# Eight key groups of the relu pass moved into the last head steps of the large pass

## What is computed

```python
x = x + xattn0(ln(x), ctx, Wq, Wkv, Wo, bo)       # 16 heads of 64 over 12544 context rows
x = x + band_attn(ln(x), ...)                     # self attention within a band
x = x + experts0(ln(x), ...)                      # 8 experts, the best 2
x = x + xattn1(ln(x), ctx, mask, W, b)            # below
x = x + scan(ln(x), ...)
x = x + experts1(ln(x), ...)                      # 32 experts and 2 shared ones

def xattn1(input, context, mask, W, b):           # the relu pass
    q = relu(input @ W.T + b)
    k = relu(context @ W.T + b)
    scores = where(mask, -inf, q @ k.T)
    return softmax(scores) @ k
```

## Time and profile before

| | us |
|---|---|
| median of 3 runs | 1534.51 |
| lowest and highest | 1531.64, 1535.97 |
| profiled execution | 1531.62 |
| its span, first to last instruction | 1529.9 |

### The profile page before, as it was taken

The page is one execution under the profiler, slowest core; times in us unless marked ns, Lnnn a source line. Parts: engine busy times, 40 slices in busy tenths (PEclk is TensorE's granted clock), DMA queues, the critical chain, the costliest instruction groups (busy, mean ns, idle before and its releaser), DMA issues. The chain is left out here.

```text
span 1529.9 us, 24927 instructions
## 1 busy us (share of the span) xinstructions
PE 1467.8 (96%) x9257; PEld 1272.2 (83%) x9257; DVE 1084.1 (71%) x2051; ACT 832.6 (54%) x1581; POOL 598.7 (39%) x517
## 2 busy tenths in 40 slices
PE   8999999999999999999999999999987979999769
PEld 6888888888888888888888888888875869999648
DVE  5777777777777777777777777777787337777784
ACT  4555566556555565556656566556652136666221
POOL 5243433434343434343434343343310245666240
PEclk9999999999999999999999999999999799999899
DMA  5000000000000000000000000000004221221720
GB/s 186 1 25 1 1 25 1 25 1 25 1 25 1 25 1 25 1 25 1 25 1 20 6 1 25 1 1 1 1 28 179 83 105 55 82 82 34 302 104 4
DMA packets 11099, 58.92 MB, mean 39 GB/s; under 512 B 2330, under 2 KB 4707, under 8 KB 9956
## 3 DMA queue, kind: packets, MB, share of 16 engines
q1 hardware_dynamic: 10980, 57.33, 10.0%
HBM read 57.19 MB, written 0.13 MB: 37 GB/s over the span
## 5 line engine op out<-in xcount | busy, mean ns | idle before, releaser
L487 DVE TENSOR_TENSOR pT<-ps,pT 128x896 fp32r<-128x896 f32 x224 | 244.5, 1091 | 203.8 <-ACT pT L396 203.8
L317 POOL CAST V<-Vraw 128x512 fp32r<-128x512 f32 x189 | 115.7, 612 | 651.1 <-ACT Vraw L402 550.5
L396 ACT ACTIVATE pT<-ps 128x896 fp32r<-128x896 f32 x224 | 205.9, 919 | 179.4 <-PE ps L562 178.6
L402 ACT COPY Vraw<-ps 128x512 f32<-128x512 f32 x189 | 110.9, 587 | 266.0 <-PE ps L544 266.0
L318 POOL TENSOR_TENSOR V<-Vraw,V 128x512 fp32r<-128x512 f32 x189 | 242.7, 1284 | 15.1
L433 DVE TENSOR_REDUCE nmx<-ps 128x1 f32<-128x896 f32 x224 | 242.0, 1080 | 0.0
L380 ACT ACTIVATE prob<-ps,nm 128x896 f32<-128x896 f32 x224 | 223.8, 999 | 0.0
L620 PE MATMUL ps<-ident,prob 128*128 128x128 f32 x1568 | 214.2, 277 | 8.7 <-ACT prob L380 4.5
L575 PEld LDWEIGHTS ps<-pT,V 128*128 128x128 f32 x1568 | 215.0, 188 | 8.1 <-issue 0.3
L575 PE MATMUL ps<-pT,V 128*128 128x256 f32 x1568 | 220.3, 280 | 0.0
L620 PEld LDWEIGHTS ps<-ident,prob 128*128 128x128 f32 x1568 | 167.5, 140 | 17.0 <-ACT prob L380 9.2
(11 more groups left out here) (312 smaller groups left out, 2426.7 us busy)
## 6 DMA issues: line engine op xcount, KB each, us to landing
raw<-in_ctxT SPq DMA_DIRECT2D x14, 896.0 KB, 4.4
d_raw<-in_ctxT SPq DMA_DIRECT2D x14, 896.0 KB, 4.6
w<-in_w SPq DMA_DIRECT2D x2, 4096.0 KB, 18.1
wg<-in_wg SPq DMA_DIRECT2D x1, 4352.0 KB, 17.8
wu<-in_wu SPq DMA_DIRECT2D x1, 4352.0 KB, 27.6
wd<-in_wd SPq DMA_DIRECT2D x1, 4352.0 KB, 36.3
e_ea<-in_alog SPq DMA_DIRECT2D x1, 2048.0 KB, 7.8
d_mrow<-in_mask SPq DMA_DIRECT2D x14, 112.0 KB, 4.5
```

Source lines behind the costliest of these rows:

```text
L317: link(pool, nc.gpsimd.tensor_copy(v_high(g, i), by_head(Vraw[:, j % 2, :])), "pool_chain")
L396: nc.scalar.activation(pT[u % 2][:, :, 0, :], pT_ps, ACT.Copy).then_inc(sem("pTh_ready"), 1)
L487: nc.vector.tensor_tensor(pT[u % 2][:, :, 1, :], pT_ps, pT[u % 2][:, :, 0, :].bitcast(F32), ALU.subtract).then_inc(sem("pTl_ready"), 1)
```

## The change

Eight of the 56 key groups of the relu pass (those of chunks 0 and 1) are made at the end of the large pass, with its own split chunks: chunks 0 and 1 are loaded and split once more as its chunks 14 and 15, the latter in quarters. Six groups go into bank 6 in steps 216 to 219, 222 and 223, the last two into banks 2 and 3 behind the projection and behind the last turned heads. For this the relu weights are loaded and split at the start of the kernel, with `Vraw` as the buffer, and `d_kT` becomes a ring of four. The relu pass starts with group 8 and has 13 groups before round 0, then three per round in rounds 0 to 8 and four in rounds 9 to 12. Chunks 2 and 3 are loaded in the band stage and split by GpSimd in the expert stage, where chunk 0 and the weights were; chunks 4 and 5 are loaded there. In the relu pass the first three turns of tiles come before groups 10 to 12, and VectorE's casts of the first keys before its other first work. Some constants are built later or in another place, `afc` is loaded in the band stage, and the numbers of spins change: 9 more in the band stage, 2 fewer in the first expert stage, 3 fewer in the last. The scan takes two buffers from `d_kT`.

```diff
@@ stage_context
+    LG = 2 * KT
+    later_at = [steps - 8, steps - 7, steps - 6, steps - 5, steps - 2, steps - 1]
+        wx_first = Vraw[:, 0, :].rearrange("p (k n) -> p k n", k=KT)
...
+                sp.dma_start(wx_first, t["wx"]).then_inc(sem("wx_early"), 16)
+                sp.dma_start(v["bx"][:, :], t["bx"]).then_inc(sem("wx_early"), 16)
...
-                for c in range(1, chunks):
+                for c in range(1, chunks + 2):
                     sp.wait_ge(sem("cT_split"), 2 * c)
-                    sp.dma_start(raw[:, :, :], t["ctxT"][c]).then_inc(sem("rawT_in"), 16)
+                    sp.dma_start(raw[:, :, :], t["ctxT"][c % chunks]).then_inc(sem("rawT_in"), 16)
...
+                pool.wait_ge(sem("wx_early"), 32)
+                link(pool, nc.gpsimd.tensor_copy(v["d_wxh"][:, :, :], wx_first), "pool_chain")
+                nc.gpsimd.tensor_tensor(v["d_wxl"][:, :, :], wx_first, v["d_wxh"][:, :, :].bitcast(F32),
+                                        ALU.subtract).then_inc(sem("wx_split"), 1)
                 split_context(1)
...
-                    elif u % H0 == H0 - 2 and u // H0 + 2 < chunks:
+                    elif u % H0 == H0 - 2:
                         split_context(u // H0 + 2)
+                split_quarters(chunks + 1)
@@ stage_context, ScalarE
+                def later_keys(G, bank):
+                    act.wait_ge(sem("dk_done"), G + 1)
+                    act.wait_ge(sem("wx_early"), 32)
+                    m, cols = (G % LG) // 2, slice((G % 2) * HK, (G % 2 + 1) * HK)
+                    nc.scalar.activation(v["d_kT"][G // LG][:, m, cols], ps[:, bank, 0:HK], ACT.Relu,
+                                         bias=v["bx"][:, m:m + 1], scale=1.0).then_inc(sem("dkT_ready"), 1)
...
+                    if u in later_at:
+                        later_keys(later_at.index(u), 6)
                     if u + 1 < steps:
                         exp_step(u + 1)
@@ stage_context, TensorE
+                    if u in later_at:
+                        pe.wait_ge(sem("o_added"), u - 1)
+                        pe.wait_ge(sem("vraw_ready"), len(v_steps))
+                        later_keys(later_at.index(u), 6)
                     p = u + AHEAD
...
+                        if u in later_at:
+                            pe.wait_ge(sem("dkT_ready"), later_at.index(u) + 1)
                         weighted_sum(u - 1)
...
                         project(range(0, 4))
+                        later_keys(6, 2)
...
                 weighted_sum(steps - 1)
                 turn_heads((4, 5, 6), 7)
+                later_keys(7, 3)
@@ stage_relu_context
-    done = [max(early, ahead)]
+    early, done = 8, [13]
+    SKIP = 2
     for c in range(chunks):
         left = chunks - 1 - c
-        share = -(-(groups - done[-1]) // left) if left > 0 else 0
+        share = (groups - done[-1]) // left if left > 0 else 0
...
+                for n in range(3):
+                    turn_keys(0, n)
                 for G in range(before, done[0]):
-                    relu_keys(nc, pe, sem, v, G, ps[:, G % 2, 0:HK])
-                for n in range(NG):
-                    if n == 3:
-                        pe.wait_ge(sem("dkNl_ready"), 1)
-                    turn_keys(0, n)
+                    keys(G)
                 pe.wait_ge(sem("dq_split"), 1)
                 scores(0)
+                pe.wait_ge(sem("dkNl_ready"), 1)
+                turn_keys(0, 3)
@@ stage_mix0, GpSimd
+                for i in range(2):
+                    pool.wait_ge(sem(f"dctx_in{i}"), 16)
+                    nc.gpsimd.tensor_copy(v["d_cTh"][i][:, :, :], v["d_raw"][i][:, :, :]).then_inc(sem("dcTh_ready"), 1)
+                    pool.wait_ge(sem("dcTh_ready"), i + 1)
+                    nc.gpsimd.tensor_tensor(v["d_cTl"][i][:, :, :], v["d_raw"][i][:, :, :],
+                                            v["d_cTh"][i][:, :, :].bitcast(F32), ALU.subtract).then_inc(sem("dcTl_ready"), 1)
-                v["spin"](8, 3)
+                v["spin"](6, 3)
@@ stage_band, TensorE (before the waits for o1, o1T and o2T)
+                v["spin"](3, 0)
+                v["spin"](3, 0)
+                v["spin"](3, 3)
@@ stage_mix1
-                v["spin"](8, 0)
+                v["spin"](5, 0)
```

More of the change, by code:

```diff
@@ L129, in build @@
         norms = (norm_vector, norm_pool, norm_tensor)
+        keep("bx", [P, KT])
+        keep("d_wxh", [P, KT, D], F32R)
+        keep("d_wxl", [P, KT, D], F32R)
+        v["d_kT"] = [sb(f"d_kT{i}", [P, KT, CK]) for i in range(2)]
         stage_context(nc, t, sb, sem, link, ps, norms, v)
+        keep("tri", [P, P])
+        keep("below", [P, E1, E1])
+        keep("afc", [P, KT, D])
+        keep("wx", [P, KT, D])
         keep("wg0", [P, KT, E0])
@@ L578, in weighted_sum, with later_keys @@
                     mm.then_inc(sem("pv_done"), 1)
+                def later_keys(G, bank):
+                    c = chunks + G // LG
+                    if G == 0:
+                        pe.wait_ge(sem("wx_split"), 1)
+                    if G % LG == 0:
+                        pe.wait_ge(sem("cT_split"), 2 * c + 2)
+                    if 0 < G < len(later_at):
+                        pe.wait_ge(sem("dkT_ready"), G)
+                    relu_keys(nc, v, G % LG, cTh[c % 2], cTl[c % 2], ps[:, bank, 0:HK]).then_inc(sem("dk_done"), 1)
                 def turn_heads(pairs, bank):
@@ L870, in stage_scan @@
         inv = [sb(f"e_inv{i}", [P, W], F32, own) for i in range(2)]
-        g = [sb(f"e_g{i}", [P, W], F32, own) for i in range(2)]
+        g = [x[:, :, :].rearrange("p k n -> p (k n)")[:, 0:W] for x in v["d_kT"][0:2]]
         def cn(x):
@@ L1084, in first_use @@
         return next((c for c in range(chunks) if done[c + 1] > KG * C), None)
-    to_split = {c: [C for C in range(chunks) if KG * C >= done[0] and max(first_use(C) - 1, 0) == c]
-                for c in range(chunks)}
+    to_split = {c: [C for C in range(2 + SKIP, chunks) if max(first_use(C) - 1, 0) == c] for c in range(chunks)}
     with ExitStack() as own:
@@ L1138, in load_mask @@
                         sem(f"dmask_in{c % 2}"), 16)
-                load_mask(0)
-                load_mask(1)
-                masks = 2
-                for C in range(v["early_loads"], chunks):
-                    if C >= 2:
-                        sp.wait_ge(sem("dcTl_ready"), C - 1)
-                    sp.dma_start(raw[C % 2][:, :, :], t["ctxT"][C]).then_inc(sem(f"dctx_in{C % 2}"), 16)
-                    if C >= 2 and masks < C - 1:
+                masks = 0
+                for C in range(4 + SKIP, chunks):
+                    split_in = next(c for c in range(chunks) if C - 2 in to_split[c])
+                    while masks <= split_in + 1:
                         load_mask(masks)
                         masks += 1
+                    sp.wait_ge(sem("dcTl_ready"), C - 1 - SKIP)
+                    sp.dma_start(raw[C % 2][:, :, :], t["ctxT"][C]).then_inc(sem(f"dctx_in{C % 2}"), 16)
                 for c in range(masks, chunks):
@@ L1165, in _ @@
                 norm_pool(pool, 3)
-                for C in range(split, (done[0] + KG - 1) // KG):
-                    split_low(C)
                 for g in range(KG):
@@ L1209, in exp_step @@
                                          accum_out=rs[:, b:b + 1]).then_inc(sem("dexp_done"), 1)
-                act.wait_ge(sem("wx_in"), 32)
-                for C in range(split, (done[0] + KG - 1) // KG):
-                    split_high(C)
                 before = min(early + 2, done[0])
@@ L1230, in _ @@
                         keys(G)
-                    if c > 0:
-                        for C in to_split[c]:
-                            split_high(C)
+                    for C in to_split[c]:
+                        split_high(C)
                     for n in range(2):
@@ L1243, in _, with keys_high @@
             def _(dve):
+                def keys_high(c):
+                    if c >= 1:
+                        dve.wait_ge(sem("ds_done"), c)
+                    for g in range(KG):
+                        dve.wait_ge(sem("dkT_ready"), KG * c + g + 1)
+                        nc.vector.tensor_copy(part(kTh, g), part(kT[c % ring], g)).then_inc(sem("dkTh_ready"), 1)
                 norm_vector(dve, 3)
+                keys_high(0)
                 nc.vector.memset(U[:, :], 0.0)
@@ L1251, in _ @@
                                         ALU.subtract).then_inc(sem("dq_split"), 1)
-                def keys_high(c):
-                    if c >= 1:
-                        dve.wait_ge(sem("ds_done"), c)
-                    for g in range(KG):
-                        dve.wait_ge(sem("dkT_ready"), KG * c + g + 1)
-                        nc.vector.tensor_copy(part(kTh, g), part(kT[c % ring], g)).then_inc(sem("dkTh_ready"), 1)
                 def rows_low(c, n):
```

136 lines of the change are left out of this document (68 added, 68 removed).

## The result

| kernel | median us | lowest to highest | ratio to the kernel before, 95% |
|---|---|---|---|
| before (beside it) | 1535.24 | 1531.64 to 1537.58, 4 runs | |
| changed | 1520.74 | 1519.71 to 1525.08, 4 runs | 0.9917 [0.99, 0.9934] |
| before, beside the second measurement | 1534.63 | 1533.72 to 1538.33, 7 runs | |
| changed, measured again later | 1525.44 | 1523.14 to 1527.0, 4 runs | 0.9933 [0.9916, 0.9949] |

By the ratios the change is faster by 0.7 to 0.8%; between the medians lie 14.5 us in the first measurement and 9.2 in the second. The forecast was 11.5 us and 1523.0. The profiled execution took 1521.6 (span 1519.5).

The account below looks back on a forecast made before the run. TensorE was taken to bound the relu rounds, with holes in the large pass's last steps. +6.9 - 6.4 - 9.8 - 1.5 - 0.7 = -11.5 us took the profiled 1531.6 to 1520.1; plus 2.9, median 1523.0, range 1515 to 1530.5.

Parts of the forecast that it names:

- TensorE bounds the relu rounds: Relu pass, rounds 0 to 8 with three groups: TensorE still ends last, each of eight rounds gives 1.22 us, -9.8 us.
- The 0.2 us to spare: Relu rounds: margin by which VectorE's casts and GpSimd's subtractions of the keys end before TensorE wants them.
- rival 2: Relu rounds: VectorE's chain takes the round over, each round gives only 0.5 us, 1528.8 us in all; chance 0.16.
- Start of the relu pass, -6.4: Relu pass up to round 1: first transposes of probabilities 6.65 us earlier, about 0.3 us of waiting; bounds -4 and -8.
- Rival 3's first half: Round 0's 3 us stand: the clock falls, some 4.9 us run at half speed, +2.4 us; whole rival's chance 0.17.
- Steps 216 to 219, +0.8: Large pass: groups 0 to 3 make these steps look like steps with values, +0.8 us; bounds 0 and +3.
- Last steps, +5.6: Large pass from step 222: groups 4 to 7 partly exposed with their relus, +5.6 us; bounds 3.0 and 8.8.
- The lock in steps 220, 221, +0.5: Large pass around step 220: GpSimd splits the last chunk while VectorE scales sums from two SBUF operands, +0.5 us (0 to 1.5).
- Band and expert stage, -1.5: Spins may bring the clock back, but GpSimd's split of two chunks delays the ranking: -1.5 us, bounds -3.6 and +1.4.
- the two forms that the forecast took from it: Port lock shared with GpSimd: VectorE takes it for casts within SBUF and for two SBUF inputs.
- the first row (2.29 us): Expert stage, evidence for the lock: one scalar operation stood 2.29 us against GpSimd.
- Last stage, -0.7: Five spins for eight: the three are worth 1.4 us if the norm waits for them, nothing if not; -0.7 us.

Follow-up runs that it names:

- the run with two products: Changed kernel with the third product (weights high by context low) left out of the relu pass's key groups: 10.87 us a round of three, 11.54 of four.

## Why the prediction was right, and where it was not

- **TensorE bounds the relu rounds: right to the size.** -9.80 us for -9.8. The 0.2 us to spare were 0.18 us of waiting already, and the whole chain had 0.4 us of room: taking the upper end of the bounds (10 us) was right by less than the text suggests. With one group less a round, rival 2's chain would have set it, as the run with two products shows. What was close was GpSimd's subtractions, which ended 7.18 us into the round (forecast 7.1), and not VectorE's casts: put at 3.2 us and an end at 5.0, they took 1.29 and ended at 2.83. Here all four were through before GpSimd's second subtraction; it was the first subtraction that waited for them, 1.84 us for some 1.15.
- **Start of the relu pass, -6.4: measured -5.9.** The first transposes came 7.11 us nearer (forecast 6.65), with the stand of 2.72 us where "some 3 us" were foreseen. Rival 3's first half then took 1.4 us back: the clock does fall behind that stand in most executions. Its place was right, its price (2.4) too high. With the clock up the term was -7.3 us (26.25 for 33.53 from first group to round 1).
- **Steps 216 to 219, +0.8: measured +0.71,** and with two thirds of the work taken out still nothing less than the 19.4 of before: they are holes. The forecast's own sum here gives +0.6, not +0.8 (20.6 less 0.6 is 20.0, for 19.41).
- **Last steps, +5.6: measured +4.72.** The mis-sized terms: group 4 was put at 1.15 and came to 0.70; from the transposes of 223 to the end 4.0 us were added and 4.4 forecast. The lower bound, 3.0 us with all holes used, is what banks of their own gave: 3.02.
- **The lock in steps 220, 221, +0.5: measured +0.07.** GpSimd's quarters did meet VectorE's two-operand steps, as forecast. The two scalings of the sums took 0.56 and 0.53 us beside GpSimd's four casts, and 0.27 and 0.29 two steps later without them (timeline). But most of it went into VectorE's own wait behind them, 0.31 us in the kernel before (second fence) and none now, so that TensorE's two steps grew by 0.07 us: the lock was there, but hardly on the path.

```profile
1144.79 2.13 POOL L314 CAST cTh<-raw 128x448 fp32r<-128x448 f32 x4 [18.79 <-PE ps L567]
...
1145.94 0.56 DVE L488 TENSOR_TENSOR U<-U 128x128 f32<-128x128 f32 x1
1146.54 0.53 DVE L490 TENSOR_TENSOR U<-U,rden 128x128 f32<-128x128 f32 x1
```

```profile
1146.27 1.09 DVE L487 TENSOR_TENSOR pT<-ps,pT 128x896 fp32r<-128x896 f32 x1 [0.31 <-ACT pT L396]
```

- **Band and expert stage, -1.5: measured -2.71, but by luck of the clock.** Over its eight executions the stage took 69.1 us in the mean, 0.5 below the one of the kernel before; at the same clock of 0.88 it took 71.73 us for 69.65. Two slips of the forecast's sum lie here: three spins at 0.47 us are 1.4 us and not 1.3, and the eight before the norm ended at 1201.6, not 1201.4. The forecast had the ranking behind GpSimd until 1215.5 and a third down product not before 1215.9, in a stage it let start earlier. The mechanism is shown: 9.73 us of ranking became 0.67 without GpSimd. Its price was 1.0 us. That the same kind of wait would also meet the norm (0.6 us), because the constants moved into GpSimd's queue right behind its norm step, was missed; the text priced those constants at nothing, at the place they left, and not at the place they came to.
- The Trainium skill ("SBUF — State Buffer", Who interferes with whom) gives the exclusive port lock for more than the two forms that the forecast took from it: `tensor_scalar` can take it as well as copies and casts, beside the instructions with two SBUF inputs. The trace agrees: a step with two SBUF inputs took 4.01 us against 3.98 us of GpSimd's subtraction, and 0.22 without it. The norm's `xn`, which is a `tensor_scalar`, took 1.26 against 0.41 us, and the first row (2.29 us) is of that form too.
- **Last stage, -0.7: measured +1.26.** The term was right at equal clock (-0.9); the clock cost 2.3 us. The term was priced without the clock.
- **Scan, 0: measured +0.81,** and 0.8 to 2.1 us over the twelve executions. The forecast had no term for it, and its cause is open.
- **The sum** of -11.5 met -10.0 between the profiled executions (1521.6 for 1531.6) and -14.5 and -9.2 between medians. That the term for the groups is right is shown apart from the clock: tail, start and rounds give 5.50 - 5.92 - 9.80 = -10.2 us for the forecast's -9.3, and the changed kernel without the band's spins is 10.4 us below the kernel before. Right for the right reasons there. That the whole came so near is in part luck: the first profile had its stage at the best clock of eight, and the scan's loss and the last stage's stood against it. What the spins do the forecast did not know.

## What to carry to other kernels

Work of a full engine moved into another stage is cheap only where a hole stands ready for it. Four groups cost 0.7 us in steps that each had one; the four in the last steps cost 4.7, of which 1.7 was a shared buffer and a follow-up ahead of the other engine's critical operation. Give such work buffers of its own and put its follow-up behind that operation. When a step is moved, price it where it arrives: what runs beside it there, and whether it shares a port with the engine that matters. And compare stretches at equal granted clock: here one execution told stages of 20 to 90 us to 0.1 us where the clock was full, and only to several us where it fell.

## What was not expected of the hardware

- In the band and expert stage the same instructions in the same order took from 66.94 to 74.16 us, by where the clock fell and for how long; the summed loss (one less the clock, over stretches of one microsecond) was 1.7 us in the best and 11.9 in the worst.
- Spins alone, in a kernel otherwise unchanged, were worth 0.5% (0.995 [0.9933, 0.9966]); in the changed kernel those of the band and expert stage gave nothing that the times show.
- VectorE steps of 0.22 us on 64 columns lasted 4.01, 1.70 and 4.02 us beside GpSimd instructions of 3.98, 1.68 and 3.98 us: here the wait was as long as the other engine's whole instruction, eighteen times the own one.
- It also goes the other way: where VectorE's casts came first, GpSimd's subtraction lasted 1.84 us for 1.15.
